# Cross-attention and a ternary feed-forward on one core: the attention product read from PSUM, pair sums in their own buffer, maxima transposed in f32

## What is computed

```
x, ctx: (16, 256, 512) f32;  W1: (2048, 512);  W2: (512, 2048)
q = layernorm(x);  k = v = ctx              # 8 heads over the 256 rows, 32 rows a head
qk[h] = q[h].T @ k[h] / sqrt(32)            # 512 x 512 for each head and batch
a[h]  = v[h] @ softmax(qk[h], axis=-1).T
x = x + a
h = silu(bitlinear(layernorm(x), W1));  x = x + bitlinear(h, W2)
# bitlinear: activations quantised to int8 levels per row, weights to -1, 0, 1
```

## Time and profile before

| | before |
|---|---|
| median of 3 runs | 945.06 us (943.43 to 946.72) |
| the profiled execution, its own time | 945.5 us |
| its span in the profile | 943.5 us |
| TensorE busy | 801.0 us, 85% |
| VectorE busy | 801.2 us, 85% |
| ScalarE busy | 672.2 us, 71% |
| GpSimd busy | 612.8 us, 65% |
| mean granted TensorE clock | 0.966 |

### The profile page before, as it was taken

One profiled execution on the slowest core, in us unless ns is written; L12 is line 12 of the kernel. 1 busy time (PEld: TensorE's weight loads), 2 busy tenths in 40 slices (PEclk: granted clock), 3 DMA queues, 4 the chain that ended last, 5 costly groups with the idle time before them and its releaser, 6 DMA issues.

```text
span 943.5 us, 17275 instructions
## 1 busy us (share of the span) xinstructions
PE 801.0 (85%) x4580; PEld 295.1 (31%) x4580; DVE 801.2 (85%) x1624; ACT 672.2 (71%) x1089; POOL 612.8 (65%) x619
## 2 busy tenths in 40 slices
PE   1658898898899899998899889998899999998875
PEld 0413233333333333332333333332333333333222
DVE  2958999998999899998999899998999999998542
ACT  3577677777777677776777777776777787777753
POOL 4134676776677666775777667775776678775751
PEclk9968899999999999999999999999999999999987
DMA  8540333331233333330333333321333333221000
GB/s 274 173 133 1 68 80 79 80 68 42 60 67 79 79 79 78 67 78 24 66 79 78 79 79 67 78 46 45 79 79 78 79 78 68 57 46 34 23 11 23
DMA packets 49912, 67.97 MB, mean 72 GB/s; under 512 B 6336, under 2 KB 30912, under 8 KB 49344
## 3 DMA queue, kind: packets, MB, share of 16 engines
q1 hardware_dynamic: 49856, 67.39, 29.4%
HBM read 33.55 MB, written 8.39 MB: 44 GB/s over the span
## 4 chain that ended last, share of the span: by engine, by line
PE 45%; DVE 29%; issue 15%; POOL 4%; DMA 2%; ACT 2%; SPq 1%; DVEq 1%; POOLq 0%; ACTq 0%
PE bank_b L937 11%; DVE mx L717 7%; PE pv L906 7%; PE mxp L896 7%; DVE late L791 6%; PE st L886 6%; DVE hmx L796 3%; PE bank_a L975 3%; PE bank_a L927 3%; PE bank_b L975 3%; POOL late L496 2%; DVE sm L770 2%; DVE cparts L722 2%; DMA qs<-ql 1%; PE bank_a L945 1%
## 5 line engine op out<-in xcount | busy, mean ns | idle before, releaser
L469 POOL TENSOR_TENSOR probs<-probs 128x512 f32<-128x512 f32 x256 | 328.4, 1299 | 150.3 <-PE pv L906 99.5
L717 DVE TENSOR_REDUCE mx<-mxp 128x1 f32<-128x512 f32 x512 | 338.5, 681 | 69.5 <-PE mxp L896 54.6
L555 ACT ACTIVATE probs<-st,sm 128x512 f32<-128x512 f32 x512 | 343.0, 685 | 55.7 <-PE st L886 53.3
L896 PE MATMUL mxp<-ks,qs 96*128 96x512 f16 x512 | 203.3, 398 | 52.7 <-DMA qs<-ql 25.0
L886 PE MATMUL st<-qs,ks 98*128 98x512 f16 x512 | 200.0, 392 | 6.4 <-DMA qs<-crow 4.3
L906 PE MATMUL pv<-probs,vt 128*32 128x512 f32 x1024 | 145.2, 640 | 0.0
L937 PE MATMUL bank_b<-w2t,late 128*128 128x512 f16 x512 | 135.4, 389 | 2.6 <-ACT late L587 2.6
L886 PEld LDWEIGHTS st<-qs,ks 98*128 98x128 f16 x512 | 50.3, 98 | 149.5 <-ACT probs L555 78.9
L896 PEld LDWEIGHTS mxp<-ks,qs 96*128 96x128 f16 x512 | 53.9, 105 | 126.0 <-DVE mx L717 58.0
L796 DVE TENSOR_REDUCE hmx<-late 128x1 f32<-128x512 f32 x128 | 84.6, 682 | 2.2
L618 ACT ACTIVATE late<-bank_a,sm 128x512 f32<-128x512 f32 x64 | 44.0, 687 | 59.3 <-PE bank_a L975 59.3
(11 more groups left out here) (92 smaller groups left out, 1034.7 us busy)
## 6 DMA issues: line engine op xcount, KB each, us to landing
xs<-x SPq DMA_DIRECT2D x32, 256.0 KB, 3.8
cs<-ctx SPq DMA_DIRECT2D x32, 256.0 KB, 3.8
ks<-kh SPq DMA_DIRECT2D x64, 128.0 KB, 3.4
qs<-qh SPq DMA_DIRECT2D x64, 128.0 KB, 3.8
xr<-x SPq DMA_DIRECT2D x32, 256.0 KB, 3.4
out<-late SPq DMA_DIRECT2D x32, 256.0 KB, 2.0
probs<-w SPq DMA_DIRECT2D x4, 1024.0 KB, 8.4
ks<-kl SPq DMA_DIRECT2D x32, 128.0 KB, 3.2
```

The lines of the kernel that those rows point to most:

```text
L469: pool.tensor_tensor(probs[:, 2 * pair, h, :], probs[:, 2 * pair, h, :], probs[:, 2 * pair + 1, h, :], ALU.add).then_inc(sum_done, 1)
L555: act.activation(probs[:, c, h, :], st[u % 2][:, :], ACT.Exp, scale=sm1[:, r, ESC:ESC + 1]).then_inc(exp_done, 1)
L717: dve.reduce_max(mx[:, slot.ring(off), NC * h + c:NC * h + c + 1], mxp[m % 2][:, :], axis=AX.X).then_inc(max_done, 1)
L896: pe.matmul(mxp[m % 2][:, :], qs[0:3 * DH, r, h, c * P:(c + 1) * P], ks[0:3 * DH, r, h, :], start=True, stop=True).then_inc(mx_done, 1)
```

## The change

Four things change. (1) `attend` on VectorE reads the attention product straight from its PSUM bank `pv`; ScalarE's copy `pvs` is gone, and the bank is given back when `attend` is done. (2) The pair sums go to a buffer `sums` of their own, no longer over `probs`; they wait for the exponentials and for the last tile's `denominators`, and no more for `values`. The exponentials wait for `values` and the pair sums of the last tile, chunk by chunk. (3) The maxima are transposed as f32 (`mx` is 128 wide for each ring place, the columns behind the 16 maxima zeroed once), ScalarE copies the high f16 part from the bank, and VectorE makes the low part by subtracting that from the bank (`ct_low`); two transfers of one row each take the place of one of two rows. (4) The plan: `values` at 8, 11, 15, 18 in place of 6, 10, 15, 18; `ct` at -5 (unit 11) in place of -4 (unit 12); `ct_low` at -4; and `key_scale_b` is a `tensor_scalar` with a per-partition scalar in place of a `scalar_tensor_tensor`.

```diff
...
     vt_evac=[-7],
-    cparts=[-6],
-    ct=[-4],
+    ct=[-5],
     ct_evac=[-5],
-    values=[6, 10, 15, 18],
+    ct_low=[-4],
+    values=[8, 11, 15, 18],
     sums=[6, 7, 8, 9, 14, 15, 16, 17],
     denominators=[12, 19],
-    pv_evac=[18],
     invert=[20],
...
     invert_c=[21],
-    cparts_low=[-6],
     hidden_scale_b=[35],
...
           'xn2', 'sums'],
- 'act': ['kh', 'vt_evac', 'tanh', 'ct_evac', 'qh', 'pv_evac', 'ht_evac', 'rescale', 'key_squares', 'xqt_evac',
+ 'act': ['kh', 'vt_evac', 'tanh', 'ct_evac', 'qh', 'ht_evac', 'rescale', 'key_squares', 'xqt_evac',
          'quantise_act'],
- 'dve': ['max_read', 'key_scale_b', 'cparts', 'norm2', 'cparts_low', 'aggregate', 'hidden_scale',
+ 'dve': ['max_read', 'key_scale_b', 'norm2', 'ct_low', 'aggregate', 'hidden_scale',
          'hidden_scale_b', 'attend', 'hidden_scale_c', 'norm2b', 'absmax2', 'invert_b', 'key_scale',
...
         probs = sb("probs", [P, NC, TH, D], f32)
-        pvs = sb("pvs", [P, 2, D], f32)
+        sums = sb("sums", [P, 2, TH, D], f32)
         dspread = sb("dspread", [P, D // DH, DH], f32)
...
         w2t = sb("w2t", [P, FG, D], f16)
-        mx = sb("mx", [P, RING, UNITS], f32)
-        cparts = sb("cparts", [P, RING, 2, UNITS], f16)
-        crow = sb("crow", [2 * UNITS, 2, P], f16)
+        mx = sb("mx", [P, RING, P], f32)
+        crow = sb("crow", [UNITS, 2, 2, P], f16)
         bn1 = sb("bn1", [P, RING, 6], f32)
...
         max_done = sem("max_done")
-        cpart_done = sem("cpart_done")
         ct_done = sem("ct_done")
         ct_evac = sem("ct_evac")
+        ct_low = sem("ct_low")
         vt_done = sem("vt_done")
         pv_done = sem("pv_done")
-        pv_evac = sem("pv_evac")
         sum_done = sem("sum_done")
...
                     r, k = slot.ring(1), slot.ring(1) % 2
-                    wait(sp, ct_evac, slot, 1, 1, 1)
-                    sp.dma_start(qs[3 * DH:3 * DH + 2, r, :, :].rearrange("o h m -> o (h m)"), crow[:, k, :]).then_inc(c_stacked[r], 16)
+                    wait(sp, ct_low, slot, 1, 1, 1)
+                    for a in range(2):
+                        sp.dma_start(qs[3 * DH + a:3 * DH + a + 1, r, :, :].rearrange("o h m -> o (h m)"), crow[:, k, a, :]).then_inc(c_stacked[r], 16)
                 if slot.has(-2):
...
         BANK_A = uses(("key_norm", 0, key_clamped, 1, 1), ("ht", 0, ht_evac, 2, 1), ("ht", 1, ht_evac, 2, 2), ("vt", 0, vt_evac, 1, 1),
-                      ("ct", 0, ct_evac, 1, 1), ("xqt", 0, xqt_evac, 1, 1),
+                      ("ct", 0, ct_low, 1, 1), ("xqt", 0, xqt_evac, 1, 1),
                       ("first", 1, gate_done, FC, 2), ("first", 3, gate_done, FC, 4))
...
             pool.memset(half[:, :], -0.5).then_inc(consts, 1)
+            pool.memset(mx[:, :, :], 0.0).then_inc(consts, 1)
             pool.wait_ge(consts0, 2)
                                    base=0, pattern=[[-1, P]], channel_multiplier=1).then_inc(consts, 1)
-            pool.wait_ge(consts, 4)
+            pool.wait_ge(consts, 5)
             def rstd(slot, off):
...
                 if h == 0:
-                    wait_alone(pool, pv_done, slot, NC, off, 2 * pair + 1, passed)
+                    wait_alone(pool, dn_done, slot, 2, off - 1, pair + 1, passed)
                 wait(pool, exp_done, slot, UNITS, off, TH * (2 * pair + 1) + h + 1)
-                pool.tensor_tensor(probs[:, 2 * pair, h, :], probs[:, 2 * pair, h, :], probs[:, 2 * pair + 1, h, :],
+                pool.tensor_tensor(sums[:, pair, h, :], probs[:, 2 * pair, h, :], probs[:, 2 * pair + 1, h, :],
                                    ALU.add).then_inc(sum_done, 1)
             def residual(slot, off):
...
                 pool.memset(ks[3 * DH:P, :, :, :], -1.0).then_inc(consts, 1)
-                pool.wait_ge(consts, 5)
+                pool.wait_ge(consts, 6)
             weights = [(WEIGHTS["ones"][0], ones_rows, 0)]
...
                     act.wait_ge(w_t, WG)
-                if u % (2 * TH) == 0:
-
-                    wait(act, dn_done, slot, 2, -1, c // 2 + 1)
+                if h == 0:
+                    wait(act, pv_done, slot, NC, -1, c + 1)
+                wait(act, sum_done, slot, 2 * TH, -1, TH * (c // 2) + h + 1)
                 wait(act, st_done, slot, UNITS, 0, u + 1)
                 act.activation(probs[:, c, h, :], st[u % 2][:, :], ACT.Exp, scale=sm1[:, r, ESC:ESC + 1]).then_inc(exp_done, 1)
-
-            def values_evac(slot, off):
-                wait(act, pv_done, slot, NC, off, NC)
-
-                act.copy(pvs[:, slot.ring(off) % 2, :], pv[:, :]).then_inc(pv_evac, 1)
             def key_squares(slot, off):
...
             def maxima_evac(slot, off):
                 if slot.has(off - 2):
-                    act.wait_ge(c_stacked[slot.ring(off - 2)], slot.lap(off - 2, 16))
-                act.copy(crow[:, slot.ring(off) % 2, :], bank_a[0:2 * UNITS, 0:P // 2].bitcast(f16)).then_inc(ct_evac, 1)
+                    act.wait_ge(c_stacked[slot.ring(off - 2)], slot.lap(off - 2, 32))
+                act.copy(crow[:, slot.ring(off) % 2, 0, :], bank_a[0:UNITS, 0:P]).then_inc(ct_evac, 1)
             def tokens_evac(slot, off):
...
             def run(slot):
-                steps = {"pv_evac": values_evac, "ct_evac": maxima_evac, "key_squares": key_squares,
+                steps = {"ct_evac": maxima_evac, "key_squares": key_squares,
                          "kh": key_high, "qh": query_high, "ht_evac": hidden_evac, "vt_evac": values_t_evac,
...
                 wait(dve, x_k_operands, slot, Q_LOW, off, K_SCALE)
-                dve.scalar_tensor_tensor(out=sm[:, ESC:ESC + 1], in0=sm[:, KCLAMP:KCLAMP + 1], scalar=SCALE / Q_UP, in1=sm[:, INVK:INVK + 1],
-                                         op0=ALU.mult, op1=ALU.mult).then_inc(x_k_scales, 1)
+                dve.tensor_scalar(sm[:, ESC:ESC + 1], sm[:, KCLAMP:KCLAMP + 1], sm[:, INVK:INVK + 1], SCALE / Q_UP,
+                                  ALU.mult, ALU.mult).then_inc(x_k_scales, 1)
             def key_low(slot, off):
...
                 dve.reduce_max(mx[:, slot.ring(off), NC * h + c:NC * h + c + 1], mxp[m % 2][:, :], axis=AX.X).then_inc(max_done, 1)
-            def maximum_parts(slot, off):
-                r = slot.ring(off)
-                wait(dve, max_done, slot, UNITS, off, UNITS)
-                dve.tensor_copy(cparts[:, r, 0, :], mx[:, r, :]).then_inc(cpart_done, 1)
-
             def maximum_low(slot, off):
-                r = slot.ring(off)
-                wait(dve, cpart_done, slot, 2, off, 1)
-                dve.tensor_tensor(cparts[:, r, 1, :], mx[:, r, :], cparts[:, r, 0, :], ALU.subtract).then_inc(cpart_done, 1)
+                k = slot.ring(off) % 2
+                wait(dve, ct_evac, slot, 1, off, 1)
+                dve.tensor_tensor(crow[:, k, 1, :], bank_a[0:UNITS, 0:P], crow[:, k, 0, :], ALU.subtract).then_inc(ct_low, 1)
             def invert(slot, off):
...
             def attend(slot, off):
                 k = slot.ring(off) % 2
-                wait(dve, pv_evac, slot, 1, off, 1)
+                wait(dve, pv_done, slot, NC, off, NC)
                 wait(dve, token_scales, slot, T_HIDDEN, off, D_BACK)
-                dve.tensor_tensor(att[:, k, :], pvs[:, k, :], rden[:, :], ALU.mult).then_inc(token_scales, 1)
+                dve.tensor_tensor(att[:, k, :], pv[:, :], rden[:, :], ALU.mult).then_inc(token_scales, 1)
             def norm2(slot, off):
...
             def run(slot):
-                steps = {"max_read": maximum, "cparts": maximum_parts, "cparts_low": maximum_low,
+                steps = {"max_read": maximum, "ct_low": maximum_low,
                          "hidden_scale": hidden_scale, "hidden_scale_b": hidden_scale_b,
...
         def _(pe):
-            pe.wait_ge(consts, 4)
+            pe.wait_ge(consts, 5)
             def scores(slot, u):
                     if not slot.looped and slot.b == 0:
-                        pe.wait_ge(consts, 5)
-                    pe.wait_ge(c_stacked[r], slot.lap(0, 16))
+                        pe.wait_ge(consts, 6)
+                    pe.wait_ge(c_stacked[r], slot.lap(0, 32))
                 wait(pe, exp_done, slot, UNITS, 0, u - 1)
...
                     wait(pe, vt_evac, slot, 1, off, 1)
-                    wait(pe, pv_evac, slot, 1, off, 0)
+                    wait(pe, token_scales, slot, T_HIDDEN, off - 1, ATTENDED)
                 for h in range(TH):
...
                 for h in range(TH):
-                    last = pe.matmul(dn[DH * h:DH * (h + 1), :], ones[:, 0:DH], probs[:, 2 * pair, h, :],
+                    last = pe.matmul(dn[DH * h:DH * (h + 1), :], ones[:, 0:DH], sums[:, pair, h, :],
                                      start=(pair == 0), stop=(pair == 1), skip_group_check=True)
...
             def maxima_transpose(slot, off):
-                wait(pe, cpart_done, slot, 2, off, 2)
+                wait(pe, max_done, slot, UNITS, off, UNITS)
                 bank_free(pe, BANK_A, slot, off, place("ct", 0))
```

(3 more changed lines are left out.)

## The result

The changed kernel takes 963.9 us (median of 4, 961.02 to 967.25); the kernel before, beside it on the same chips, 944.2 us (941.33 to 946.72). The ratio is 1.021, interval 1.016 to 1.026: 2.1% slower, where 0.8% was forecast. The profiled execution took 965.5 us, its span 963.7.

The account below looks back on a forecast made before the run. The prediction took a closed circle through the transfer `qs<-ql` to bound the slot at 26.21 us, with a second circle as tight. Terms 7.7 + 2.3 - 3.8 + 3.0 - 2.0 gave +7.2 us, hence 952.3 us, range 927 to 964.

Parts of the forecast that it names:

- The bound: Slot set by a circle through `qs<-ql`: `kl`, maximum 0, `first`, `max_read` 5, `kl`; 7.54 + 3.89 + 3.94 + 10.84 = 26.21 us.
- `values` moved: `values` step 1 behind maximum 0 lengthens maximum 0 to `first`: +0.32 us per looped slot, +0.63 in written-out slots.
- The transpose in f32: Transpose of the maxima on TensorE in f32 takes 0.1 us more than in f16, between 0 and 0.3.
- `kl` held: GpSimd's earlier pair sum 0 holds VectorE's `kl`, which ends 0.12 us later per slot, between 0 and 0.3.
- The credit for `key_scale_b`: VectorE's new `key_scale_b` form takes 0.76 us off each of five first slots behind a jump, -3.8 us in all.
- The second gap in unit 6: With `values` 0 moved away, TensorE stands still about 0.75 us before `second` 0; the transfer's circle doesn't pass here.
- a rival in which the level falls in every slot: TensorE's new idleness lowers its clock each slot, doubling at least `values` 1's 1.03 us: +28 us, 981 us; chance 0.04.
- The ends: Slots before the loop save about 1.5 us, the last ones some 0.5 us, as the transfer isn't waited for: -2.0 us.
- small terms: Bounds in the forecast's own case: f32 transpose 0 to 0.3 us, hold of `kl` 0 to 0.3, ends 0 to -5.
- the forecast's own case: The transfer's circle still binds and lengthens: 952.3 us, 0.8% slower, 946 to 962 with small terms at bounds; chance 0.49.
- signs of being wrong: Slot under 26.0 us, maximum 0 not waiting, `xqt` waiting for `ct_low`, or matmuls of 0.57 us and more mid-turn.
- The faster rival: The transfer doesn't bind, the second circle decides, and `kl` to maximum 0 is under 7.0 us: 921 us; chance 0.27.

Follow-up runs that it names:

- the fastest kernel: Changed kernel with ScalarE's copy `pvs` kept, `values` at 6, 10, 15, 18 and `kl`'s transfer issued last: 896.72 us, ratio 0.952.

## Where the prediction was right, and which of its terms failed

- **The bound.** Right: a closed circle through `qs<-ql` sets the slot. That the four pieces add up to the slot shows nothing by itself, since they always do. What shows it is the wait by name, with `kl` to maximum 0 at 7.5 to 7.6 us in the usual slots of every kernel that waits there, whatever its slot (25.46, 25.66, 26.52, 26.73), and that the slot falls when the transfer comes early and nothing else is in the way (25.64 to 24.78). With `values` 1 behind the transfer VectorE's 73 freed us are worth nothing in the usual slot: 26.52 us without them, 26.73 with them.
- **`values` moved** (+0.32 in 24 slots, +0.63 in the last four: 10.2 us) is the term that failed by its size. The run with step 1 alone moved measured 18.8 us (963.17 against 944.41), 17.9 of them in the profiled span: start 3.9, loop 9.8, three written-out slots 3.8, the rest 0.3. Forecast were 0, 7.7, 1.9 and 0.6. Three things were missed. The price of 1.03 us was read at `values` 0 in unit 6; step 1 costs 1.13 where it now stands. Behind a jump the transfer came late before as well, with 3.63 us from maximum 0 to `first`, so that this slot had less air: after the change it is 4.40, a slot of 27.05 against 26.27. And at the start the prediction held that the transfer isn't waited for; in the run with this edit alone maximum 0 waits 1.95 us for it at 105.75.
- **The transpose in f32** was put at +0.1 and costs 0.14 (4.35 against the 4.21 of the run with `values` 1 alone).
- **`kl` held**: direction and mechanism right, 0.22 instead of 0.12 us a slot. Sum 0 started a little later against `kl` than taken (614.03, 0.88 us ahead of it, not 0.98).
- **The credit for `key_scale_b`** (-0.76 in five slots) rests on a misreading. The 971 ns of the earlier trace rows are a maximum; before the change the step takes 0.91 to 0.97 us in three of the five slots with a jump and 0.33 in the other two:

```profile
436.31 1.94 PE L906 MATMUL pv<-probs,vt 128*32 128x512 f32 x8
...
441.68 0.97 DVE L705 SCALAR_TENSOR_TENSOR sm<-sm 128x1 f32<-128x1 f32 x1
...
549.07 0.33 DVE L705 SCALAR_TENSOR_TENSOR sm<-sm 128x1 f32<-128x1 f32 x1
```

  The three are those of 29.3 to 29.5 us, whose granted clock fell to 0.94 behind the jump; there the step meets GpSimd's `ql`, which it doesn't in the two of 28.1. In these two, `first` to the next `kl` takes 15.97 and 15.98 us, after the change 15.87 to 16.09: the new form gains nothing there. The mean falls, from 16.78 to 15.96, because the clock no longer falls behind any of the five jumps; why it doesn't, no run shows. Four of these slots take 28.78 us against a mean of 28.90 before, 0.12 less where 0.44 less was forecast; in the fifth the clock fell in unit 6, ahead of the jump, and it takes 29.80.
- **The second gap in unit 6** was forecast at 0.75 us and is 0.75. Its danger was named only as a rival in which the level falls in every slot (0.04); the sum put it at nothing. The level fell in one slot of the loop and in two of the three written-out ones, which are 27.74 and 27.65 us where the first, at full speed, is 26.50:

```profile
829.23 0.39 PE L884 MATMUL mxp<-ks,qs 96*128 96x512 f16 x1 [0.52 <-DVE mx L710]
830.10 0.61 PE L915 MATMUL bank_a<-idh,late 128*128 128x128 f16 x8 [0.48 <-DVE sm L692]
...
831.82 1.89 PE L925 MATMUL bank_b<-w2t,late 128*128 128x512 f16 x4 [0.68 <-ACT late L580]
```

- **The ends** (-2.0 us) were a guess of the wrong sign: +1.2 at the start, and +2.0 at the end, where +0.2 was forecast. The 13.0 us between +7.2 and +20.2 are: start 2.7, end 1.8, written-out slots 2.6 (the falls), slots with a jump 2.6, slots behind one 5 x 0.35 = 1.7, and the fourteen others 1.6.
- **The range.** With its small terms at their bounds the forecast's own case reaches from about 944 to 964 us, not from 946 to 962 as written. The 963.9 us lie at its upper end, and one of the signs of being wrong came: matmuls at the lower clock inside a turn (1.68 us for four products at 203.50).
- **The faster rival** (0.27) stayed out for the reason given: `kl` to maximum 0 stayed over 7.0 us. In the fastest kernel it is below: 6.62 us (573.45 to 580.07, a maximum 0 without a wait).
- **What the text had wrong without paying for it:** it costed the own sums only as a loss at `kl` and `attend`'s length as a property of its operands. The buffer alone is worth 22 us (2.5%), shortens `attend` without the PSUM read, and frees `cparts_low`, which stands in the second circle.

So the gain of the change was real and was spent. The bank is given back only when `attend` is done, in unit 6, which speaks against `values` 0 in that unit; no run tried it there. `values` 1 didn't have to leave unit 10 for it, as the run at 8, 10, 15, 18 shows. From the version with the copy (926.51) to that with `values` 0 in unit 8 and the bank read (939.31) it costs 13 us, from there to `values` 1 in unit 11 another 25.

What stays open: why the clock falls at the third of three equal stops, or behind a jump, in one slot and not in another. The length of the stop doesn't tell: behind stops of 2.01 to 2.24 us at the jumps of the changed kernel it never fell, and with pair sum 0 a unit later it fell behind all five, of 2.01 to 2.35. The start of the program (2.7 us over the forecast) and its end (1.8) are measured and not explained. And the own sums with the values plan of before and `kl`'s transfer last, without the split, were not run; they may be faster still.

## What to carry to other kernels

Find the closed circle, then ask of every moved instruction on which side of the wait it lands: here 1 us of work was free ahead of the transfer's landing, and behind it was paid in every round. Two circles of one length hide each other's worth: an edit that does little alone (the transfers' order, -0.5%) gave 3.2% once the other circle was shorter. When an instruction takes 1.76 us at the median and 0.68 at the least, look at what runs beside it before rewriting it; moving its neighbour may be the cheaper cure.

## What the runs showed of the hardware

- A VectorE instruction of 128x512 with two SBUF operands that started while GpSimd added ended 0.55 us behind it: 606.34 against 605.79 before, 615.84 against 615.29 after, 592.58 against 592.03 with own sums. One of 16 elements ended 0.04 us behind (613.08 against 613.04). `attend` took 0.68 us when it started after the sum, and 679 ns in the mean with a PSUM operand.
- TensorE's granted clock fell from the upper level (2.4 GHz) to the lower (1.2 GHz) in some slots, behind stops of 0.52, 0.48 and 0.68 to 0.75 us within some 3 us; four products then took up to 1.89 us instead of 1.03, and the slot 1.2 to 1.7 us more. In looped slots without a jump the lengths and windows show it only where `values` 0 had left unit 6; in the last written-out slot it came with `values` 1 alone moved as well, behind a stop of 1.94 us (28.25 us at a granted clock of 0.94). In slots with a jump it came in the kernel before too, behind a stop of 2.28 us: 29.3 to 29.5 us at 0.94 in three of five, 28.1 at 1.00 in two.
- Six transfers of 128 KB took SyncE 0.55 to 0.68 us each to issue. Their order decided 30 us in 926 with the circles shortened, and 4 us in the kernel before.
